# Shared expert's result evacuated by ScalarE and added in DRAM, adjacency sum split between three engines, other order at both ends

## Time and profile before

| what | value |
| --- | --- |
| runs of the kernel before | 1064.3, 1066.85, 1068.14 us, median 1066.85 |
| profiled execution | 1066.63 us, its span 1064.8 us |
| busy of the span | PE 918.4 us (86%), DVE 577.8 (54%), ACT 487.4 (46%), POOL 437.2 (41%) |
| traffic | HBM read 101.55 MB, written 47.20 MB |

### The profile page before, as it was taken

One profiled execution on the slowest core, in us unless ns is written; L12 is line 12 of the kernel. 1 busy time (PEld: TensorE's weight loads), 2 busy tenths in 40 slices (PEclk: granted clock), 3 DMA queues, 4 the chain that ended last, 5 costly groups with the idle time before them and its releaser, 6 DMA issues.

```text
span 1064.8 us, 21255 instructions
## 1 busy us (share of the span) xinstructions
PE 918.4 (86%) x4604; PEld 495.4 (47%) x4605; DVE 577.8 (54%) x1320; ACT 487.4 (46%) x993; POOL 437.2 (41%) x348
## 2 busy tenths in 40 slices
PE   3258698879787999999999999999999999999994
PEld 1143354545343555554545545555544554545542
DVE  5958898889764443446343454444455454453321
ACT  5276563742132443446444454444455454463331
POOL 2011101110032455555655554645545565655643
PEclk8569888798888999999999999999999999999998
DMA  5211120111338578777887778687887787876654
GB/s 170 75 41 52 40 87 7 40 43 40 102 107 268 117 165 178 164 170 206 186 199 145 176 164 218 125 205 176 179 207 173 220 181 210 184 168 122 122 103 72
DMA packets 90267, 149.25 MB, mean 140 GB/s; under 512 B 9648, under 2 KB 46768, under 8 KB 90224
## 3 DMA queue, kind: packets, MB, share of 16 engines
q0 software_dynamic: 33120, 80.64, 38.6%
q1 hardware_dynamic: 57104, 68.13, 19.5%
HBM read 101.55 MB, written 47.20 MB: 140 GB/s over the span
## 4 chain that ended last, share of the span: by engine, by line
PE 47%; issue 9%; DVE 5%; ACT 4%; DVEq 3%; ACTq 3%; DMA 1%; SPq 0%; POOL 0%; POOLq 0%
PE bank L258 40%; PE bank L1484 4%; PE bank L1475 3%; ACT gu L240 3%; DVEq L1170 2%; ACTq L1170 2%; DVE gu L247 1%; DMA stage_dn<-in_L_ffn_w_down_dram 1%; DVE hid L1400 1%; DVE dn L250 1%; DVE hT L1409 1%; ACT silu L1263 0%; PE bank L1456 0%; ACTq L240 0%; DVE mark_p L400 0%
## 5 line engine op out<-in xcount | busy, mean ns | idle before, releaser
L258 PE MATMUL bank<-gu,xgT 128*128 x1764 | 408.6, 382 | 11.9 <-issue 7.6
L1213 POOL DMA_INDIRECT out_dram<-y,ids_i x145 | 242.2, 1671 | 283.4 <-DMA out_dram<-y,ids_i 156.9
L258 PEld LDWEIGHTS bank<-gu,xgT 128*128 128x128 f16 x1764 | 173.1, 98 | 193.7 <-issue 22.9
L258 PE MATMUL bank<-dn,hT 128*128 x870 | 212.1, 380 | 15.9 <-issue 15.8
L1201 POOL DMA_INDIRECT xg<-xrows,ids_i x153 | 158.8, 1038 | 64.2 <-issue 41.4
L1400 DVE SCALAR_TENSOR_TENSOR hid<-bank,xg,silu 128x256 f32<-128x256 f32 x146 | 70.3, 482 | 207.3 <-ACT silu L1263 207.3
L1275 ACT CAST hT<-bank 128x256 f16<-128x256 f32 x146 | 53.7, 368 | 224.9 <-PE bank L1475 224.9
L1282 ACT ACTIVATE y<-bank 128x512 f32<-128x512 f32 x145 | 86.6, 597 | 133.5 <-PE bank L258 133.5
L1409 DVE TENSOR_TENSOR hT<-bank,hT 128x256 f16<-128x256 f32 x146 | 61.7, 423 | 150.7 <-ACT hT L1275 150.7
L258 PEld LDWEIGHTS bank<-dn,hT 128*128 128x128 f16 x870 | 85.0, 98 | 90.6 <-issue 23.3
L247 DVE SCALAR_TENSOR_TENSOR gu<-stage_gu,gu (+1 forms) x64 | 75.6, 1222 | 48.1 <-ACT gu L240 48.1
(11 more groups left out here) (217 smaller groups left out, 770.2 us busy)
## 6 DMA issues: line engine op xcount, KB each, us to landing
stage_gu<-in_L_ffn_w_gate_dram SPq DMA_DIRECT2D x32, 512.0 KB
stage_gu<-in_L_ffn_w_up_dram SPq DMA_DIRECT2D x32, 512.0 KB
stage_dn<-in_L_ffn_w_down_dram SPq DMA_DIRECT2D x32, 512.0 KB
x_sb<-in_x_dram SPq DMA_DIRECT2D x4, 1024.0 KB, 6.9
xrows<-adj SPq DMA_DIRECT2D x4, 1024.0 KB, 4.2
out_dram<-acc SPq DMA_DIRECT2D x4, 1024.0 KB, 4.7
xg<-xrows,ids_i POOLq DMA_INDIRECT x153, 4.4
out_dram<-y,ids_i POOLq DMA_INDIRECT x145, 5.1
```

The source lines that it names most:

```text
L258: last = nc.tensor.matmul(out_ap, stationary(a, c), moving(w, c), start=(c == 0 and (a, w) == parts[0]), stop=(c == chunks - 1 and (a, w) ...
L1213: g_.indirect_dma_start(out, bass.IndirectOffsetOnAxis(ap=ids_i[:, t:t + 1], axis=0), y[:, t % YS, :], None, compute_op=ALU.add).then_inc( ...
```

## The change

- `s_add` on VectorE is replaced by `s_result` on ScalarE: the shared tile is written from PSUM over the batch's `acc`, once the store of that `acc` has landed. `add_shared` on POOL then adds the four tiles to the stored rows in DRAM by one accumulating transfer of 1 MB. SP stores `acc` right behind the normalised rows.
- In the adjacency sum, ScalarE scales the masked sigmoids by g/2 into `under` (`scaled_adjacency`), POOL adds that to `acc`, VectorE adds the transposed tile from PSUM times g/2 to `acc`. `tmp` and the loop of line 978 go.
- Order at the start: constants are cast first, the search follows the first guess at once, coefficients (`gains`) come behind the counts of `bound(0)`; ScalarE counts before its sigmoids. `convert_low(0)` is moved from between `bound(0)` and `update(0)` to ahead of `low_rows(0)`, both conversions of number 1 behind the last search step and the second silu. All of `x_stats(1)` stands in `update(0)`.
- Order at the end: `s_gate_up(3, 1)` whole behind ranks and columns; in the second block `copy_table` ahead of `s_high(3, 3)`, expert 1's high parts behind the shared results; `tab` and `onehot` in f16.
- `routing` does in one instruction what it did in four, in three places.

```diff
-        tab = early("tab", [P, B, 2, P])
+        tab = early("tab", [P, B, 2, P], F16)
...
-        def s_add(dve, b, i):
-            dve.wait_ge(S["s_down"], RT * b + i + 1)
-            a = acc[:, RT * b + i, :]
-            nc.vector.scalar_tensor_tensor(a, bank[DB[i]][:, :], 1.0 / W_SCALE, a, ALU.mult, ALU.add).then_inc(S["added"], 1)
+        def s_result(act, b, i):
+            act.wait_ge(S["s_down"], RT * b + i + 1)
+            act.wait_ge(S[f"out_stored{b}"], 16)
+            nc.scalar.activation(acc[:, RT * b + i, :], bank[DB[i]][:, :], ACT.Identity, scale=1.0 / W_SCALE).then_inc(S["added"], 1)
+        def add_shared(pool, b):
+            pool.wait_ge(S["added"], RT * (b + 1))
+            nc.gpsimd.dma_start(out[b * N:(b + 1) * N, :].rearrange("(i p) h -> p i h", p=P), acc[:, b * RT:(b + 1) * RT, :],
+                                accum_op=ALU.add).then_inc(S["shared_added"], 16)
...
                     store_rows(b - 1)
-                    if b >= 2:
-                        store_out(b - 2)
+                    store_out(b - 1)
                     store_shares(b - 1)
...
                     if b >= 1:
                         for c in range(SC):
                             s_low(pool, b - 1, c)
+                    for i in range(RT):
+                        a = acc[:, b * RT + i, :]
+                        pool.wait_ge(S["adj_scaled"], RT * b + i + 1)
+                        pool.wait_ge(S["base_ready"], RT * b + i + 1)
+                        nc.gpsimd.tensor_tensor(a, under[:, i, :], a, ALU.add).then_inc(S["half_ready"], 1)
+                    if b >= 1:
+                        add_shared(pool, b - 1)
...
                     else:
                         sum_marks(pe, p)
-                        s_gate_up(pe, b, 1, (0,))
                         rank_tokens(pe, b)
                         count_columns()
-                        s_gate_up(pe, b, 1, (1,))
+                        s_gate_up(pe, b, 1)
                         turn_found(pe, p)
...
+                def scaled_adjacency(b):
+                    for i in range(RT):
+                        act.wait_ge(S["adj_ready"], RT * b + i + 1)
+                        nc.scalar.activation(under[:, i, :], adj[:, i, :], ACT.Identity, scale=gcol[:, 3:4]).then_inc(S["adj_scaled"], 1)
...
+                for k in range(STEPS):
+                    counts(0, k, range(DVE_TILES, RT))
                 act.wait_ge(S["small_loaded"], 3 * 16)
                 nc.scalar.activation(gcol[:, 1:2], gcol[:, 0:1], ACT.Sigmoid).then_inc(S["gamma_ready"], 1)
                 sigmoids(0)
-                for k in range(STEPS):
-                    counts(0, k, range(DVE_TILES, RT))
...
                     if more:
                         mixed(b + 1)
+                    scaled_adjacency(b)
                     if p >= 0:
                         s_high(act, p, 3)
...
+                    if p >= 0:
+                        s_result(act, p, 0)
+                        s_result(act, p, 1)
                     for i in range(RT):
                         transposed_rows(b, i)
+                    if p >= 0:
+                        s_result(act, p, 2)
...
                                          ACT.Sigmoid).then_inc(S["scores_ready"], 1)
+                    if p >= 0:
+                        s_result(act, p, 3)
                     if more:
                         counts(b + 1, 2, second)
                         sigmoids(b + 1)
-                        if p < 0:
-                            convert_high(act, 1)
                         counts(b + 1, 3, range(RT))
                         s_silu(act, b, 0)
                         counts(b + 1, 4, range(RT))
                         s_silu(act, b, 1)
+                        if p < 0:
+                            convert_high(act, 1)
...
+                def gains():
+                    inverse_stds(1, slice(1, 2))
+                    dve.wait_ge(S["gamma_ready"], 1)
+                    ch.done(v.tensor_scalar(gcol[:, 2:3], gcol[:, 1:2], -1.0, 1.0, ALU.mult, ALU.add))
+                    ch.step(v.tensor_scalar(gcol[:, 3:4], gcol[:, 1:2], 0.5, None, ALU.mult))
+                    coefficients(0)
...
-                    if b + 1 < B:
+                    if 1 <= b < B - 1:
                         x_stats(b + 1, range(0, RT // 2))
...
                     if more:
-                        x_stats(b + 1, range(RT // 2, RT))
+                        x_stats(b + 1, range(RT // 2 if b else 0, RT))
                     for i in range(RT):
+                        a = acc[:, b * RT + i, :]
                         dve.wait_ge(S["adjT_ready"], RT * b + i + 1)
-                        v.tensor_tensor(tmp[:, i, :], adj[:, i, :], bank[SIMB[i % 2]][:, :], ALU.add).then_inc(S["adjT_used"], 1)
+                        dve.wait_ge(S["half_ready"], RT * b + i + 1)
+                        v.scalar_tensor_tensor(a, bank[SIMB[i % 2]][:, :], gcol[:, 3:4], a, ALU.mult, ALU.add).then_inc(S["adjT_used"], 1)
                     dve.wait_ge(S["adjT_used"], RT * b + RT)
-                    for i in range(RT):
-                        a = acc[:, b * RT + i, :]
-                        ch.done(v.scalar_tensor_tensor(a, tmp[:, i, :], gcol[:, 3:4], a, ALU.mult, ALU.add))
-                    ch.settle()
...
                     bound(b)
-                    if b == 0:
-                        convert_low(dve, 0)
                     nth = update(b, nth)
...
                     if p >= 0:
-                        s_add(dve, p, 1)
                         find_keys(dve, ch, p)
+                    else:
+                        convert_low(dve, 0)
                     low_rows(b)
...
                         if p >= 0:
                             mark(dve, p, 2)
-                        else:
-                            convert_low(dve, 1)
...
                         search_step(b + 1, 4)
+                        if p < 0:
+                            convert_low(dve, 1)
...
                 for t in range(XG):
                     gather(t)
+                add_shared(pool, b)
                 pool.wait_ge(S["tables_ready"], 1)
-                pool.wait_ge(S["out_stored"], 16 * B)
+                pool.wait_ge(S["shared_added"], 16 * B)
...
                 s_silu(act, b, 3)
+                copy_table(act, b)
                 s_high(act, b, 3)
-                copy_table(act, b)
-                for e in range(AHEAD):
+                convert_high(act, SH)
+                for i in range(RT):
+                    s_result(act, b, i)
+                for e in range(1, AHEAD):
                     convert_high(act, SH + e)
```

58 lines of the change are left out of this document (20 added, 38 removed).

## The result

The changed kernel took 1081.08 us (median; 1080.11 to 1082.7) against 1067.08 of the kernel before, measured beside it: ratio 1.0137, 95% interval 1.0114 to 1.016. So the change costs 11 to 14 us. I had forecast 1068.9, no change; the range ended at 1076.

What follows compares the result with a forecast made beforehand. It took a ring of waits between VectorE's search, ScalarE's counts and TensorE's products to bound the middle stage. Shifts -4.8 + 5.1 + 2.9 + 2.2 - 2.7 - 0.4 = +2.3 gave 1068.9 us from 1066.6; range 1058 to 1076.

Steps and rivals of the forecast that it cites:

- Search start and select 0, -3.1 and -5.9: Start: search begins 3.1 us earlier, and batch 0's adjacency multiply (line 964, the post "select") 5.9 us earlier.
- -4.8 at the normalised rows: Batch 0: with all four x_stats ahead of the PSUM sums, 1.1 us more, similarities and normalised rows come 4.8 us earlier.
- It starts at 91.3: End of batch 0: third gate/up product starts at 91.3, not 92.98, but cold, 2.5 us longer; line 964 at +0.3.
- Turns 1 and 2, +2.9 and +2.2: Batches 1 and 2, from one start of line 964 to the next: 2.9 and 2.2 us longer.
- base of the next batch, now behind POOL's accumulating transfer, falls beside the routing and I add 0.4 for contention: POOL in batches 1 and 2: the later base costs 0.4 us by line 911 (the post "bound").
- The wait behind the scores: Batches 1 and 2: ScalarE waits 4.11 us for the fourth shared product, delaying search step 2's second counts by 4.2.
- The slower rival: POOL's additions between line 314 and the sums run long: 1081 at 2.12 us each, 1073.5 at 1.5; chance 0.22.
- The last turn, -2.7: Last batch: ranks directly behind routing, then 24 products in 5.3 us, gain 2.3; shared adds ahead of find_keys, 0.4 more.
- The tail, -0.4: Tail: last shared down products end 1.45 us earlier though cold (12.7 us); later second-expert conversion costs 1.1; net -0.4.
- The tiles, 0: Stage from 326.0 us to the end, 738.8 us: the change leaves its code alone, so its length stays.
- the two signs that I had named as proof of an error: ScalarE's wait behind the scores not met on VectorE, or line 964 of batch 1 still 2 us ahead of 107.05.
- the other signs: Among others: line 911 of batch 1 near 91.2, last ranks right behind routing without 5 us idle, first routed product near 328.

Runs made afterwards that it cites:

- a_conv1: Changed kernel with both conversions of the shared weights' second half back in their old places; 1076.12 us, ratio 1.007.
- c_again: The changed kernel as it is, measured once more beside the kernel before; 1079.72 us, ratio 1.0104.
- p_start: Kernel before with the start's order alone changed, both moved conversions and x_stats included; 1068.35 us, ratio 0.9998.
- a_base: Changed kernel with POOL's accumulating transfer of each batch issued one batch later, behind the next base; 1075.25 us, ratio 1.0067.
- s_gate: Kernel before with ScalarE's shared results, POOL's accumulating transfers, and last-turn ranks and column counts ahead of the whole second gate/up product; 1074.28 us, ratio 1.0066.
- a_gate: Changed kernel with the first half of the last batch's second gate/up product back ahead of its rank product; 1078.44 us, ratio 1.0093.
- a_noadj: Changed kernel with the adjacency sum as before, on VectorE alone without ScalarE scaling or POOL addition; 1072.66 us, ratio 1.0039.
- p_adj: Kernel before with the adjacency sum alone split over ScalarE, POOL and VectorE as in the change; 1075.42 us, ratio 1.0073.
- j_first: Kernel before with the adjacency split alone, POOL's four additions ahead of the last low part; 1067.68 us, ratio 0.9988.
- h_start: Kernel before with end part except ranks' order, ScalarE's result and accumulating transfer for batch 2 alone, start part without moved conversions; 1056.24 us, ratio 0.9885.
- a_four: Changed kernel with fourth shared result and POOL's transfer later, second-half conversions back, half the last gate/up product ahead of ranks; 1064.83 us, ratio 0.9959.
- h_last: Kernel before with end part except the ranks' order, ScalarE's result and accumulating transfer for batch 2 alone; 1057.46 us, ratio 0.9894.
- a_five: Changed kernel with fourth result and transfer later, conversions back, half product ahead of ranks, POOL's additions ahead of last low part; 1059.89 us, ratio 0.9908.

## Why the prediction was wrong

**Search start and select 0, -3.1 and -5.9: right.** Measured -2.5 and -5.4.

**-4.8 at the normalised rows: -2.7.** I had put POOL's additions of batch 0 at 1.13 without a cost to VectorE. They took 5.74 for four, and the adjacency multiply beside them 3.75 for 2.73.

**"It starts at 91.3" (select 1 at +0.3): 94.61, and select 1 at +3.9.** The direction was right (a later start, an idle of 6.08, a cold product of 8.13), the start 3.3 too early: 2.1 from the line above, the rest from ScalarE's sigmoids, which waited 1.89 for the rows' store where I had allowed a few tenths. a_conv1 shows the conversions' place to be worth 3.8 of the turn's 9.3 (2.1 against c_again's turn 0 of 68.4); p_start alone has +7.9. The early search was paid back in the turn, as forecast, and more.

**Turns 1 and 2, +2.9 and +2.2: +5.8 and +6.5. This is the step that failed.** Here lie 7.2 of the 12.2 us by which the profiled shift (+14.5) missed the forecast (+2.3). Against its own turn, in turn 1 and turn 2, the similarities came at +2.4 and +2.4 (forecast +2.1), search step 2 at +5.5 and +5.8 (forecast +4.2), and bound at +7.0 and +7.3 (forecast +3.8, to which 0.4 for contention comes). From search step 2 to bound the forecast lets the path shrink by 0.4 and it grew by 1.5 in both turns. The sentence "base of the next batch, now behind POOL's accumulating transfer, falls beside the routing and I add 0.4 for contention" is the term of wrong size: a_base puts it at 2.2 in turn 1. I had named that POOL's transfer stands ahead of the base and had not followed the base to what it then lies beside. The wait behind the scores, forecast at 4.11 by TensorE's product, was there in kind: ScalarE idled 3.60 in turn 1 and 4.84 in turn 2. Why search step 2 was 1.3 and 1.6 later than forecast is not shown in full; in turn 1 the similarities ran 5.27 and not 4.42, but in turn 2 4.70 and not 4.92, and in c_again 4.59 and 5.32, so their length is not an effect of the change. The slack that I let select eat, 0.9 and more, was there (+7.0 at bound, +5.8 at select; +7.3 and +6.5).
The slower rival had the right time (1081) for a wrong reason: the additions took 1.23 each in these turns, 1.44 in batch 0, not 2.12.

**The last turn, -2.7: +0.9. The second step that failed, 3.6 us.** "TensorE's idle falls to about 2 us, so the 24 products take 5.3" was 5.53 and 7.30. (The terms given there, 274.95 + 1.9 + 5.7, make 282.55 and not 282.7.) The idle ahead of the ranks is not the rest of an old wait; it is the time of routing, which the split product used to fill. s_gate and a_gate show it. Also, the split costs 3.2 us in this turn (a_noadj's 48.2 against 51.4; 2.2 against c_again), where I had 1.0.

**The tail, -0.4: -0.1,** with the cold down products as forecast (12.7), here 12.99 at a granted clock of 0.81 and behind an idle of 3.57:
```profile
323.95 12.99 PE L258 MATMUL bank<-dn,s_hT 128*128 128x512 f16 x48 [3.57 <-POOL s_hT L314]
...
324.00:337.00 13.00, 12.94 (x48) 5.18 (x48) 3.40 (x3) 3.26 (x6) 9.42 (x8) 0.81 0.75 256
```
**The tiles, 0: -2.5.** This stays open: over all profiled executions the tiles are shorter where the first routed product comes late (736.3 behind 343.0, 741.5 behind 318.2), with exceptions (736.0 behind 326.6). No run separates a cause from chance.

Neither of the two signs that I had named as proof of an error came true: ScalarE's wait was met on VectorE, and select 1 did not stay ahead. Of the other signs, bound of batch 1 (94.47 for 91.2), the idle ahead of the ranks and the first routed product (343.04 for 328) were off.

## What to carry to other kernels

Work moved off the busiest engine is priced by what is queued behind it on the engine that receives it, and by what that then lies beside: here five changes of place with the same work decided between +1.0 to +1.4% and -0.9%. Two edits that each remove the same wait don't add, and one of them may have been the other's filler. Where an engine has idle time in one turn of a loop only, move the work in that turn only.

## What the runs showed of the hardware

- Behind an idle time the same 12 TensorE products took 4.73 us (5.76 idle, granted clock 0.57, p_adj) or 2.75 (2.41 idle, j_first). The length of the idle time alone does not decide it: in the last turn the 12 products behind the ranks took 2.76 us in h_start (1.66 idle ahead of the ranks, clock 1.00) and in a_four (1.18 idle, 1.00), but 4.45 in h_last (1.65 idle, 0.61) and in a_five (1.18 idle, 0.61). Over all slow stretches read here the granted clock lay at 0.54 to 0.81, so part of each ran at the lower level, 1.2 GHz. A difference of 1.7 us in a single profile can be this alone:
```profile
281.19 4.73 PE L258 MATMUL bank<-xT,gu 128*128 128x512 f16 x12 [5.76 <-DVE acc L319]
```
```profile
274.68 2.75 PE L258 MATMUL bank<-xT,gu 128*128 128x512 f16 x12 [2.41 <-DVE acc L319]
```
- A tiny VectorE instruction can lose several times its own length to a POOL neighbour: 128x4 elements took 0.70 us for 0.16 beside POOL's base. The adjacency multiply, four tiles of 128x512, took 3.75 for 2.74 beside POOL's additions. POOL's f32 + f32 addition of 128x512 took 1.26 us at the median, and the accumulating transfer of 1 MB landed 9.2 us after its issue, which took POOL 1.4:
```profile
L579 POOL TENSOR_TENSOR acc<-under,acc x16: 1258/1264/1723, 42.5 to 259.5; 128x512 f32<-128x512 f32 x16
...
L324 POOL DMA_DIRECT2D out_dram<-acc x4: 1302/1390/1571, 153.8 to 337.9; - x4
...
DMA to landing us min/median/max: 8.8/9.2/10.0
```
